# A three-part decoder layer on one core: batch 0's values computed in attention, and buffers kept over both borders between its phases

## The reference, cut to what matters

```
x1  = layernorm(x + attn(x))            # causal, 16 heads of 32, scores times a gate per head
x2  = layernorm(x1 + retention(x1, ctx))
      # K = xpos(ctx W_K), V = ctx W_V, Q = xpos(x1 W_Q); 16 heads with decay;
      # each head normalised; times silu(x1 g_w + g_b); then out_w
out = layernorm(x2 + ffn(x2))           # 1408 wide, gated; activations and weights
      # rounded to 8-bit integers, one scale for all of x2, one for all of h
```

## Time and profile before

| what | us |
|---|---|
| median of the 3 runs shown | 1979.34 |
| the runs | 1953.56, 1984.73, 1979.34 |
| the profiled execution, its own time | 1960.79 |
| its span, first to last instruction | 1959.0 |
| attention, to the barrier | 0 to 1038.1 |
| retention, to the barrier | 1038.1 to 1668.0 |
| feed-forward | 1668.0 to 1959.0 |

### The profile page before, as it was taken

One profiled execution on the slowest core, in us unless ns is written; L12 is line 12 of the kernel. 1 busy time (PEld: TensorE's weight loads), 2 busy tenths in 40 slices (PEclk: granted clock), 3 DMA queues, 4 the chain that ended last, 5 costly groups with the idle time before them and its releaser, 6 DMA issues. The chain is left out here.

```text
span 1959.0 us, 34998 instructions
## 1 busy us (share of the span) xinstructions
PE 1727.6 (88%) x12594; PEld 816.5 (42%) x12594; DVE 1409.5 (72%) x2524; ACT 1040.1 (53%) x1836; POOL 1151.0 (59%) x1054
## 2 busy tenths in 40 slices
PE   3988999989999799998676999999999996799895
PEld 1433344433433344343133555555555553344342
DVE  3587756787578866777644788888777776488785
ACT  3346655465555555556531566565465453465585
POOL 4057877688776786869873756656766663000044
PEclk9999999999999899999787999999999997799998
DMA  5133111221012210222214123232232111461165
GB/s 193 29 108 118 42 33 55 60 82 48 24 50 75 90 30 25 75 66 65 77 65 147 58 85 98 85 100 88 80 102 86 59 64 59 169 249 50 48 251 201
DMA packets 122661, 170.81 MB, mean 87 GB/s; under 512 B 24569, under 2 KB 72569, under 8 KB 121593
## 3 DMA queue, kind: packets, MB, share of 16 engines
q1 hardware_dynamic: 117112, 160.06, 25.3%
q10 hardware_dynamic: 5376, 8.52, 1.5%
HBM read 105.07 MB, written 38.14 MB: 73 GB/s over the span
## 5 line engine op out<-in xcount | busy, mean ns | idle before, releaser
L1030 DVE TENSOR_REDUCE a_nm<-a_mx 128x1 f32<-128x512 f32 (+3 forms) x768 | 388.8, 549 | 163.7 <-PE a_mx L1214 131.3
L1103 POOL TENSOR_TENSOR a_P<-a_P 128x512 f32<-128x512 f32 (+3 forms) x266 | 271.6, 1048 | 133.1 <-PE a_o L1243 104.5
L861 ACT ACTIVATE a_P<-a_mx 128x512 f32<-128x512 f32 (+3 forms) x470 | 213.8, 499 | 192.0 <-PE a_mx L1231 117.3
L1210 PE MATMUL a_mx<-a_Ks,a_Qs 96*128 96x512 f16 (+3 forms) x768 | 234.9, 333 | 26.7 <-DVE a_nm L1030 20.2
L1228 PE MATMUL a_mx<-a_Qs,a_Ks 128*128 128x512 f16 (+3 forms) x768 | 231.1, 336 | 25.8 <-DVE a_nm L1030 14.0
L861 ACT ACTIVATE share<-a_mx 128x512 f32<-128x512 f32 (+3 forms) x298 | 130.9, 487 | 106.4 <-PE a_mx L1231 59.9
L1103 POOL TENSOR_TENSOR a_P<-a_P,share 128x512 f32<-128x512 f32 (+3 forms) x178 | 175.0, 1011 | 16.8 <-PE a_o L1243 8.5
L2694 POOL TENSOR_TENSOR f_xr<-f_xr,f_sg 128x512 f32<-128x512 f32 x32 | 43.6, 1382 | 239.3 <-DVE f_sg L2660 199.7
L2046 PE MATMUL r_pj<-share,r_cth 128*128 128x512 f16 x512 | 163.7, 383 | 22.1 <-DVE r_ctl L1847 18.7
L2730 PE MATMUL f_pj<-f_xqT,f_wgu 128*128 128x512 bf16 x704 | 159.4, 382 | 3.2 <-ACT f_sg L2563 2.4
L2046 PE MATMUL r_pj<-r_xTh,share 128*128 128x512 f16 x512 | 158.6, 379 | 3.8 <-DVE r_xTl L1885 3.5
(11 more groups left out here) (259 smaller groups left out, 4080.8 us busy)
## 6 DMA issues: line engine op xcount, KB each, us to landing
f_xr<-x_scratch SPq DMA_DIRECT2D x64, 256.0 KB, 3.8
a_stage<-in_xT SPq DMA_DIRECT2D x24, 512.0 KB, 4.0
h_scratch<-f_h SPq DMA_DIRECT2D x3, 2816.0 KB, 9.1
f_h<-h_scratch SPq DMA_DIRECT2D x3, 2816.0 KB, 10.8
a_Ks<-a_kph SPq DMA_DIRECT2D x256, 32.0 KB, 1.9
a_Qs<-a_qph SPq DMA_DIRECT2D x256, 32.0 KB, 1.9
a_xt<-in_x ACTq DMA_DIRECT2D x32, 256.0 KB, 3.2
x_scratch<-a_xt SPq DMA_DIRECT2D x32, 256.0 KB, 2.5
```

The source lines that it names most:

```text
L861: act.activation(Pf[pf.at[key]][:, off:512], pb[:, off:512], ACT.Exp).then_inc(p_exp, 1)
L1030: dve.tensor_reduce(nm[:, col:col + 1], bank_of(it)[:, 0:n], AXX, ALU.max).then_inc(max_dve, 1)
L1103: pool.tensor_tensor(total[:, off:512], total[:, off:512], Pf[pf.at[key]][:, off:512], ALU.add).then_inc(add_pool, 1)
L1210: m = pe.matmul(pb[:, 0:n], Qs[s][0:96, j, qt * P:(qt + 1) * P], Ks[s][0:96, j, hf * 512:hf * 512 + n], start=True, stop=not diag)
```

## The change

Border of attention and retention:
- V of retention's batch 0, all 8 tiles, is made in attention (new steps "loadc", "splitc", "rv"). A ctx tile takes one of the two stage buffers, is split by ACT and DVE, and PE makes 12 matmuls of 128x512; ACT writes the result into `vr`, which is attention's value buffer V[0] and retention's V. The steps have places 14.7 to 15.82 (load) and 14.9 to 16.02 (product), and their own PE stream R. Retention loses the V products of batch 0 and the waits on them.
- Tiles 0 and 1 of ctx stay split in `cth` over the border; retention begins with the loads of tiles 2 and 3. K of tiles 0 to 3 gets a stream K0 with places -2.1 to -1.5.
- The identity, its bfloat16 copy, the ones and four row buffers are kept; retention doesn't load the identity nor cast it.
- Attention doesn't wait at its end for its x1 stores; the semaphores pass on, and retention waits for them before the residual rows ("y") and before the rows of batch 3 ("xT").

Border of retention and feed-forward:
- In the last half, each of the four output products is issued in two steps: 9 matmuls once group 2 of z is ready (stream E), and the last 3 once group 3 is.
- Retention doesn't wait at its end for its x2 stores; feed-forward waits for them before it loads its second four rows.
- The first four rows of x2 are loaded during retention, after the last context tile ("lead"), into the stage buffers, which retention uses as cst, m1 and m2.
- The sigmoids of the clip factors are made in attention (two more loads among its constants, exp on ACT, two small DVE steps). Feed-forward loads no constants; ACT's first step is a Silu on two columns. "sdr" moves to place 0.12, behind the scale's chain, and its diagonals lie in xqT[1] instead of sg[0].

The diff, cut to its core:

```diff
-CAP = {"sc": 3, "max": 3, "qk": 2, "v": 2, "wo": 2}
+CAP = {"sc": 3, "max": 3, "qk": 2, "v": 2, "wo": 2, "rv": 2}
+
+RV, RV0, RVSTEP = range(NT), 14.7, 0.16
...
+    def context(t, place):
+        key, work = ("c", t), ("rv", t)
+        def landed():
+            put("ACT", ("splitc", t), 0.65, lambda: put("DVE", ("splitc", t), 0.75, parted),
+                lambda: not t or t == 1 and has(("qk", *UNITS[LAST], "q", 0)) or room(ctx) and has(*(("stack", LAST, n, hf, j) for n in "kq" for hf in range(2) for j in range(4))),
+                lambda: t > 1 and ctx.take(key))
+        def parted():
+            stage.give(key)
+            done.add(("splitc", t))
+        def made():
+            if t > 1:
+                ctx.give(key)
+            put("ACT", work, 0.62, lambda: give_bank(work), lambda: has(("pv", 11, 0, 3)))
+        W.append((place, lambda: put("SP", ("loadc", t), 0.48, lambda: after(3.0, landed), lambda: room(stage),
+                                     lambda: stage.take(key))))
+        product(R, [place + 0.2] * 3, "rv", (t,), lambda: has(("splitc", t), ("nwlo", 1)), made)
     def policy(r):
...
+    for t in RV:
+        context(t, RV0 + RVSTEP * t)
...
+            elif kind == "splitc":
+                t = key[0]
+                i = stage.at[("c", t)]
+                w.wait_ge(x_in[i], 16 * stage.turn[("c", t)])
+                if t == 1:
+                    w.wait_ge(qk_lo, num[("qk", *UNITS[LAST], "k", 0)])
+                    w.wait_ge(qk_lo, num[("qk", *UNITS[LAST], "q", 0)])
+                elif t:
+                    for n in "kq":
+                        for hf in range(2):
+                            for j in range(4):
+                                w.wait_ge(*stacked(LAST, n, hf, j))
+                    if ctx.before[("c", t)]:
+                        w.wait_ge(rv_mm, num[("rv", ctx.before[("c", t)][1])])
+                act.activation(ctx_parts(t)[0], stageb[i][:, 0:512].rearrange("p (k t) -> p k t", k=4), ACT.Copy, scale=XS
+                               ).then_inc(c_hi, 1)
+            elif kind == "rv":
+                t = key[0]
...
-        for i in range(4):
-            w.wait_ge(x1_out[i], 16 * xt.turn[xt.now[i]])
...
+                elif name == "rv":
+                    t = key[0]
+                    if part == 0:
+                        w.wait_ge(c_lo, num[("splitc", t)])
+                        w.wait_ge(nw_lo, num[("nwlo", 1, 1)])
+                    ch, cl = ctx_parts(t)
+                    jobs = [(p[:, k, :], q[:, k, :]) for p, q, k in mm3_jobs(ch, cl, halves[2], halves[3])]
...
+        early = not b and t < 4
+        product(K0 if early else KV, [-2.1 + 0.2 * t] * 3 if early else [at_(0), at_(1), at_(2)], "K", (b, t), lambda: has(("split", b, t)), k_made)
+        if b:
+            product(KV, [at_(3), at_(4), at_(5)], "V", (b, t), lambda: has(("split", b, t)), v_made)
+        else:
...
-        product(O, places, "out", key, lambda: has(*(("zl", b, hf, g) for g in range(4))), made)
+        if (b, hf) != HALVES[-1]:
+            product(O, places, "out", key, lambda: has(*(("zl", b, hf, g) for g in range(4))), made)
+            return
+        work = ("out", *key)
+        pe_item(E, places[0] - 1.3, ("out.0", *key), 2.05, None, lambda: len(pj.busy) < pj.n and has(*(("zl", b, hf, g) for g in range(3))),
+                lambda: take(work))
+        pe_item(O, places[2], work, 0.72, made, lambda: work in pj.at and has(("zl", b, hf, 3)))
...
-    flow.order["SP"] += [("ctx", 0, 0), ("constk",), ("ctx", 0, 1), ("consts",)]
+    flow.order["SP"] += [("ctx", 0, 2), ("ctx", 0, 3), ("constk",), ("consts",)]
...
+            elif kind == "lead":
+                k = key[0]
+                w.wait_ge(c_lo, num[("split", B - 1, NT - 1)])
+                w.wait_ge(kt_mm, num[("kt", B - 1, NT - 1)])
+                w.wait_ge(kd_pool, num[("K", B - 1, NT - 1)])
+                w.wait_ge(x2_out[k], 16)
+                sp.dma_start(lead[k], x2d[k * P:(k + 1) * P, :]).then_inc(keep.lead_in[k], 16)
...
-        for k in range(4):
-            w.wait_ge(x2_out[k], 16 * len(HALVES))
...
-        put("DVE", ("sdr", 0), 0.8, lambda: done.add("diag"))
-        pe_item(T, -1.5, ("sdr",), 1.0, made, lambda: room(pj) and has("diag"), lambda: pj.take(("sdr",)))
+        put("DVE", ("sdr", 0), 0.8, lambda: done.add("diag"), lambda: has(("top", 0)))
+        pe_item(T, 0.12, ("sdr",), 1.0, made, lambda: room(pj) and has("diag"), lambda: pj.take(("sdr",)))
...
-    flow.order["SP"] += [("consts",)] + [("rows", 0, k) for k in range(4)] + [("gu", it) for it in range(IT)]
-    flow.free["SP"] = 9.5
+        done.add(("sgfree", 0, i))
+    flow.order["SP"] += [("gu", it) for it in range(IT)]
...
+                                 (cv[:, 0:1], A["clip_x"].partition_broadcast(P)), (cv[:, 1:2], A["clip_down"].partition_broadcast(P)),
...
+                    if r == 0:
+                        w.wait_ge(const_in, NCONST)
+                        act.activation(cv[:, :], cv[:, :], ACT.Exp, scale=-1.0)
...
+                if (b, hf) == (B - 1, 0):
+                    x1_stored(w)
...
-            if kind == "consts":
-                sp.dma_start(identf[:, :], A["c_ident"]).then_inc(ident_in, 16)
-                sp.dma_start(cv[:, 0:1], A["clip_x"].partition_broadcast(P)).then_inc(const_in, 16)
-                sp.dma_start(cv[:, 1:2], A["clip_down"].partition_broadcast(P)).then_inc(const_in, 16)
-                sp.dma_start(ones[:, :], A["c_ones"]).then_inc(const_in, 16)
-            elif kind == "rows":
...
-                w.wait_ge(const_in, 48)
-                act.activation(scr[:, 0:2], cv[:, :], ACT.Exp, scale=-1.0).then_inc(exp_act, 1)
+                act.activation(scr[:, 0:2], sig[:, :], ACT.Silu)
...
+class Keep:
+    def __init__(self, nc, ctx):
+        sb = lambda n, shape, dt: ctx.enter_context(nc.sbuf_tensor(n, shape, dt))
+        self.lead, self.sig = sb("lead", [P, 2 * L], F32), sb("sig", [P, 2], F32)
+        self.identf, self.identb, self.ones = sb("identf", [P, P], F32), sb("identb", [P, P], BF16), sb("ones", [P, P], F32)
+        self.rows = [sb(f"rows{i}", [P, D], F32) for i in range(4)]
+        self.x2_out = [nc.alloc_semaphore(name=f"x2o{k}") for k in range(4)]
+        self.lead_in = [nc.alloc_semaphore(name=f"lead_in{k}") for k in range(4)]
...
+            vr = ctx.enter_context(nc.sbuf_tensor("vr", [P, NT, D], F32))
+            cth0 = ctx.enter_context(nc.sbuf_tensor("cth0", [P, 8, P], F16))
+            tmp0 = ctx.enter_context(nc.sbuf_tensor("tmp0", [P, 512], F32))
+            cth1 = tmp0[:, :].bitcast(F16).rearrange("p (k t) -> p k t", k=8)
+            cth = [(cth0[:, 0:4, :], cth0[:, 4:8, :]), (cth1[:, 0:4, :], cth1[:, 4:8, :])]
+            x1_out = [nc.alloc_semaphore(name=f"x1o{i}") for i in range(4)]
+            x1_end = attention_phase(nc, A, x1d, share, keep, vr, cth, tmp0, x1_out)
+            retention_phase(nc, A, x1d, x2d, amax, share, keep, vr, cth, x1_out, x1_end, wsc, wq)
...
```

226 lines of the change are left out of this document (132 added, 94 removed).

## The result

| | before | after |
|---|---|---|
| median of 20 runs each, us | 1978.03 (1953.56 to 1991.79) | 1950.08 (1932.93 to 1970.38) |
| profiled span, us | 1959.0 | 1937.3 |

The ratio of the runs is 0.9887, with a 95% interval from 0.9858 to 0.9916: the change is worth 1.1%, some 22 us. This ratio leaves out the runs that lie more than 1.5% above the fastest of their kernel; with all twenty of each, the medians differ by 28.0 us. The two profiled executions differ by 21.7. The forecast was a gain of 33.4, to 1936.2.

What follows compares the result with a forecast made beforehand. PE was taken to bound retention and attention's output products, POOL attention's last unit, chains the borders. Terms (a) to (j) summed to +33.4 us, from a base of 1969.6 to 1936.2; range 1908 to 1962.

Steps and rivals of the forecast that it cites:

- (e): Retention's prologue: first Q product at 21.6 us after the start instead of 41.7, gain 20.1 us, bounds +10.4 and +22.
- (b): Splits of eight ctx tiles in attention's POOL-bound unit: loss 3.3 us, bounds 0 and 10; -4.2 by the skill's rule.
- (c): Eight value products in attention, the last going ahead of the first output product: loss 1.5 us, bounds 0 and -5.2.
- (f): V of tiles 4 to 7 leaves retention's units 0 to 3, DVE the next limit: gain 6.5 us, bounds +2 and +10.3.
- (a): Two more constant loads on SP in attention's prologue push the whole start: loss 1.0 us, bounds 0 and -2.
- (d): Attention's end without the wait for x1 stores; retention's start follows the last store's issue: gain 2.0 us.
- (g): Retention's last outputs in two steps, first 36 matmuls run before group 3 of z: gain 3.8 us, bounds -0.6 and +8.
- (j): sdr moved under block 0 of feed-forward: loss 0.5 us, bounds 0 and -2.
- R1: Rival: all eight value products stand before "wo" on a lower-clock PE, delaying attention; 1976.7 us, chance 0.04.
- R2: Rival: retention's prologue stays serial, gaining 10.4 us, and its units gain 2; first Q at 30 us or more; 1950.4, chance 0.22.
- R3: Rival: PE alone counts; attention's splits and products cost nothing, retention's units gain all 10.3 us; 1927.6 us, chance 0.25.
- R4: Rival: the two-step output does nothing (-0.6 us), its matmuls running at the lower clock level; 1940.6 us, chance 0.12.

Runs made afterwards that it cites:

- the run with both mended: Changed kernel, retention's second constants loaded behind context tiles 4 and 5, PE's turns of x1 rows not waiting for them: 1940.44 us, one run.
- the kernel with the PSUM source: Changed kernel, ACT's full-precision Q and K copies of attention kept in their PSUM bank, so DVE's low-half subtraction reads one PSUM source: 1940.8 us, ratio 0.9799.
- the run with six tiles: Changed kernel with splits and value products of context tiles 6 and 7 left in retention, tiles 0 to 5 in attention: 1958.24 us, ratio 0.9882.
- the kernel before with the PSUM source: Kernel before the change, with only attention's low-half subtractions reading one source from PSUM: 1965.59 us, ratio 0.9931.

## Why the prediction came out as it did

The time lay in the range, which was 54 us wide. The gain was under 2%, as the prediction had held likeliest, and it was forecast 11.7 us too large, measured by the profiled pair. The measured median, 1950.1, is 13.9 over the forecast one: 5.5 since the gain by medians was 28.0 and not 33.4, and 8.4 since the base of 1969.6 stood for a median that twenty runs put at 1978.0. By its own steps:

(e), the prologue, is where it went: 11.0 us for 20.1, the lower bound being 10.4. "Tile 3 is through at about 23", at 4.0 us per tile, took K's chain as free to run; tile 3's rotation began at 24.8 (1069.67) and its kt and S products at 28.4 and 29.8, just ahead of Q. Three things stood in it: K's first rotation could start, behind the last of K's constants, at 7.6 us and not 6.5; the splits of context tiles 4 and 5 are ahead of K of tile 2 in DVE's order, and their loads behind the bytes of the decay masks; and PE takes kt and S in order, ahead of Q. The second and a wait for constants are worth 1 to 2.4 us by the run with both mended; what the other two cost was read from the timeline and not tried. Rows 2 and 3, asked for at 15.3 by the forecast, were so at 21.2 for the same reason, behind the loads of tiles 6 and 7. I had listed each queue that the moved loads pass, but not what the loads left behind do to DVE, whose order was fixed for a landing after 3 us.

(b), the splits, cost about 0.7 and not 3.3. The row they were priced by had DVE splits lengthening POOL's adds. Six more of half the length lengthened the last unit's adds by 1.8 us, about half of the price, and moved the end by less. The Trainium skill's rule (page "SBUF — State Buffer", section "SBUF: two separate sides") was the source of the -4.2 beside it. As a price that is further off; what the traces say of the rule itself stands in the last section.

(c), the products, cost 3.5 and not 1.5; with the six splits they cost 7.4 in the kernel with the PSUM source, and the bound for the products was 5.2. One product stands behind the first output product as forecast, and the output products take 26.2 us for 24.0 from first to last; the last scaling comes 8.6 us behind them for 6.9. But in that stage POOL is waited for as soon as PE has less to do, as the run with six tiles shows. The two together, (b) and (c), cost 4.2 us against 4.8, which is luck: one was too high by what the other lacked. The other 3.5 of the 7.7 us lost in that stretch are there with two splits and no product at all. Which edit they hang on stays open (the row buffers, the stage buffers and the two splits changed together); in the kernels with the PSUM source they are 1.5. Two signs that the prediction had named: the choice of who adds didn't change, POOL making all 640 adds of attention in both profiles; and the last unit's 40 adds became 1.3 us longer in all (42.0 to 43.3), not 3.

(f) won 4.5 for 6.5, in this pair and in the one with the PSUM source; the four products put back cost 6.1 and 5.6. The prediction had DVE as the next limit. In the units after, DVE has 38.5 of 50.2 us and POOL 40.2, neither of them full, while PE has gaps; that it is POOL is argued and not shown. (a) cost 1.4 in this pair; PE's first product lies between 31.9 and 33.1 us in nine other kernels with the two loads ahead of wq and at 30.9 and 31.2 with them behind, but also at 32.0 in the kernel before with the PSUM source, which has no such loads; so (a) is known to a microsecond only.

(d), (g), (h) and (i), the ends, were right to 0.6 us: 2.4 for 2.0, 4.4 for 3.8 (3.5 by undoing it), 1.7 for 1.2, 6.7 for 6.1. All four are chains with one thing at a time, priced from rows of the same operations. (Two of their sums don't close: (d)'s 2.5 us to land and 1.8 behind it end at 1038.6 for 1038.14, and (g)'s 36 matmuls end at 1649.7, not 1649.9. Neither changes a term by more than half a microsecond.) (j) cost 1.5 for 0.5: the 2.02 us of sdr were not laid under block 0 but ahead of it.

Of the rivals, R1's mechanism (products before the output stage at the lower clock) didn't come: clock 0.95. R2's numbers came: the first Q at 30.7, which the prediction had named as its sign, (e) at 11.0 for 10.4, and a total of 1950.4 that meets the measured 1950.1 by luck, on a base too low by 8.4. Its cause came in part. It had the steps stay in series with only the four products gone, but putting these back costs 6.2 to 6.5 us and not 10.4, so the prologue wasn't a series of PE's products. What it said for itself, that the planner fixes an order with its own guess of when loads land, is what happened, on DVE and not on PE. R3 is refuted by the 4.2 us of (b) and (c) and by the PE gaps in units 0 to 3, R4 by the additions at 1.54 us.

## What to carry to other kernels

Work taken out of a serial chain is worth what the next engine's fixed order lets through: before pricing it, list for every engine what stands ahead of the next link in its queue, and when that item's own input lands. Where two executions of one kernel differ by 1 to 2%, look in the profile for single instructions many times their usual length before comparing totals; compare by stretches between instructions that both kernels have. And where POOL works without a gap beside a DVE operation, one source of that operation in PSUM keeps it from waiting; weigh against it what holding the bank costs, which here was as much as one stall.
